# Relative attention on one Trainium2 core: turn and value order, and one maximum instruction for two tiles

## The chip, the cores and the metric

The kernel runs on 1 core of one Trainium2 chip. The metric is device time in microseconds (us). The engines of a core named here are PE (TensorE: matmuls and transposes, with the weight loads as PEld), DVE (VectorE), ACT (ScalarE), POOL (GpSimd) and SP (which only issues DMAs here). Each has its own queue and takes its instructions in order; they meet only at semaphores.

## The reference

Input `x` is (4, 1024, 256). Six layers follow one another, each on a layer norm of its input:

```python
x = x + 0.5 * L0_ffn(layernorm(x))      # binarised FFN
x = x + L0_attn(layernorm(x))           # local window + latent attention
x = x + 0.5 * L0_ffn(layernorm(x))
x = x + 0.5 * L1_ffn(layernorm(x))      # ternary weight, quantised input
x = x + L1_attn(layernorm(x))           # attention with relative positions
x = x + 0.5 * L1_ffn(layernorm(x))
```

The change is in `L1_attn` alone, with 16 heads of 16 features and 1024 tokens:

```python
rp = clip(key - query, -31, 31) + 31                      # 63 buckets
attn = q @ k.T + take(q @ rpe_k_table, rp) + take(k @ rpe_q_table, rp).T
attn = softmax(attn)
out = attn @ v + segment_sum(attn, rp, 63) @ rpe_v_table
return out @ w_proj.T + b_proj
```

## The kernel before, in words

The phase is `rel_attend` (from line 1632), written as one loop of steps on each engine, `for d in range(LAST)` with 291 steps. The order of all work is the order in which these five loops are written; nothing plans it at run time. 256 steps (`ND`) carry two **query tiles** each: tile t = 2d and 2d+1 is 128 queries of one head against all 1024 keys, with the relative bias in a band around the diagonal. Eight steps make a **round**: one half of the queries (512) of four heads; there are 32 rounds. In the text, r is d modulo 8.

What each tile is for:

- *Query side.* PE writes the scores of tile t into `SP[:, t % 2, :]`, two PSUM banks for each tile (`by_query`, 2060). DVE takes the negated maximum over the 1024 keys into one column of `nm` (`top`, 1915). ACT computes exp of the band alone, 160 or 192 columns, with that maximum as bias, into `Pb` (`band`, 1858). `by_query(t)` may overwrite its half of `SP` only when `band(t - 2)` has read it (line 2070).
- *The maxima as rows.* After eight steps the 16 columns of `nm` are transposed by PE (`turn`, kind "shift", 2158), split by DVE into two f16 rows (`turn_out`, 1935 and 1937), and ACT issues four DMAs that put them as two extra rows into `Q` (`shift_rows`, 1873 to 1882). From then on the key side of that round gets scores with the maximum subtracted already.
- *Key side.* Ten steps later (`JLAG`) PE computes the same scores with keys as rows, unit q = 2(d-10) and 2(d-10)+1, into `ST`, of which there is one buffer of two banks (`by_key`, 2031). ACT takes exp of all 128x1024 into `PT` (`probabilities`, 1849). `by_key(q)` waits until `probabilities(q - 1)` has emptied `ST` (line 2038). The first unit of a round also waits for the four DMAs of `shift_rows` (line 2040).
- *Values.* Twelve steps later (`VLAG`) PE multiplies `PT`, the transposed bands `PbT` and the summed diagonals `DT` with the values, into `PV` (`values`, 2101).
- *Turns.* One PSUM bank, `T`, serves transposes. Each step `turn_band` (2017) turns the bands of step d-2 and DVE copies them out (`band_out`, 1906). Some steps have one more use of `T` (`turn_of`, 1603): "shift" at r=0, "diag" at r=4 and r=6 (POOL's diagonal sums are transposed; ACT copies them to `DT`, line 1900), "back" at r=5 (the output `XOT`, which ACT copies from `PV` at r=4, line 1893), and 36 "tail" steps for the final projection.
- *POOL* stores bands to DRAM, reads back diagonals, and sums the low part (`lower`). *SP* loads queries, keys, bias and values ahead.

Order inside a step before the change. PE (2191 to 2198): `turn_band`, `by_key` A, both `by_query`, `by_key` B, `turn`, `values`. ACT (1884 to 1902): `probabilities` A, (r=1: `shift_rows` of the round before), `band(2d)`, (r=4: `XOT`), `probabilities` B, (`DT`), `band(2d+1)`. DVE (1984 to 1990): `band_out`, `moments`, `residual`, `top(2d)`, `top(2d+1)`, `turn_out`. A and B are the first and the second key unit of the step.

Of the kernel before, what the change touches and what calls it, by code (L numbers as in the profile page):

```python
# [7 lines left out]
ALU = mybir.AluOpType  # L8
ACT = mybir.ActivationFunctionType
AX = mybir.AxisListType  # L10
P = 128
B, S, D = 4, 1024, 256
# [10 lines left out]
ONE = 16  # L23
# [25 lines left out]
def sems(nc, ctx, prefix, names):  # L49

    s = {n: nc.alloc_semaphore(f"{prefix}_{n}") for n in names.split()}

    def clear():
        with nc.Block() as block:
            @block.sync
            def _(sp):
                for x in s.values():
                    sp.sem_clear(x)
        for x in s.values():
            nc.release_semaphore(x)  # L60
    ctx.callback(clear)
    return s
# [1519 lines left out]
NSLOT = 512  # L1582
ND = NSLOT // 2
NGRP = 16
NHALF = 32
JLAG, VLAG = 10, 12
# [5 lines left out]
def tile_of(t):  # L1592

    H, i = divmod(t, 16)
    return H // 2, 4 * (H % 2) + i // 4, i % 4


def band_slot(I, c):

    return c + (0 if I == 0 else 4 if I == TPB - 1 else 8 + 4 * (I % 2))  # L1600
# [31 lines left out]
def rel_attend(nc, G, A, wpT, BDv, rvd, QKD, END, GD, PW, VD, CST):  # L1632

    with ExitStack() as ctx:
# [6 lines left out]
        nm = sb("nm", [P, 2, 16])  # L1641
# [18 lines left out]
        SP = ps("S", [P, 2, S])  # L1660
# [3 lines left out]
        s = sems(nc, ctx, "a1c", "bp_in cst_in qk_in0 qk_in1 g_in0 g_in1 v_in0 v_in1 w_in0 w_in1 zero const S max band ST exp shift_tr shift_ev "  # L1664
                 "shift_in0 shift_in1 low lowt pw0 pw1 d_in vl Tb Tb_ev PV PVb diag_tr diag_ev diag O_ev back rs norm turn turn_ev "
                 "row proj res sums stat")
# [180 lines left out]
        @block.scalar  # L1847
        def _(act):
            def probabilities(q):
                if not 0 <= q < NSLOT:  # L1850
                    return
                act.wait_ge(s["ST"], ONE + q + 1)
                if q >= 8:
                    H, j = divmod(q - 8, 16)
                    act.wait_ge(s["PV"], ONE + 8 * H + 2 * (j // 4) + 2)
                nc.scalar.activation(PT[:, q % 8, :, :], ST[:, :, :], ACT.Exp).then_inc(s["exp"], 1)  # L1856

            def band(t):
                if t >= NSLOT:
                    return  # L1860
                n, I, c = tile_of(t)
                g = t // 4
                if c == 0 and g >= 2:
                    act.wait_ge(s[f"pw{g % 2}"], 16 * (g // 2))
                    act.wait_ge(s["Tb"], ONE + 2 * (g - 1))
                    act.wait_ge(s["low"], ONE + g - 1)
                w0, w1 = (32 if I == 0 else 0), (160 if I == TPB - 1 else GW)
                col = 4 * c + I % 4
                act.wait_ge(s["max"], ONE + t + 1)
                nc.scalar.activation(Pb[:, band_slot(I, c), w0:w1], SP[:, t % 2, I * P - 32 + w0:I * P - 32 + w1], ACT.Exp,  # L1870
                                     bias=nm[:, t // 16 % 2, col:col + 1]).then_inc(s["band"], 1)

            def shift_rows(H):
                n, qh = divmod(H, 2)
                act.wait_ge(s["shift_ev"], ONE + 2 * H + 2)
                if n >= 2:
                    act.wait_ge(s["ST"], ONE + 16 * (H - 3))
                for g in range(2):
                    for e in range(2):
                        r = 64 * g + 54 + e  # L1880
                        act.dma_start(Q[r:r + 1, n % 2, qh, :, :].rearrange("r c t -> r (c t)"), mhl[:, H % 2, e, :]
                                      ).then_inc(s[f"shift_in{H % 2}"], 16)

            for d in range(LAST):
                probabilities(2 * (d - JLAG))
                if d % 8 == 1 and 9 <= d <= 8 * NHALF + 1:
                    shift_rows(d // 8 - 1)
                band(2 * d)
                if d % 8 == 4 and 20 <= d < 20 + 8 * NHALF:
                    H = (d - 20) // 8  # L1890
                    act.wait_ge(s["PVb"], ONE + 4 * H + 4)
                    act.wait_ge(s["back"], ONE + H)
                    nc.scalar.activation(XOT[:, :], PV[:, :], ACT.Copy).then_inc(s["O_ev"], 1)
                probabilities(2 * (d - JLAG) + 1)
                turn = turn_of(d)
                if turn and turn[0] == "diag":
                    k = turn[1]
                    act.wait_ge(s["diag_tr"], ONE + k + 1)
                    act.wait_ge(s["diag"], ONE + k)
                    nc.scalar.activation(DT[:, :, :].rearrange("p k q -> p (k q)"), T[:, :], ACT.Copy  # L1900
                                         ).then_inc(s["diag_ev"], 1)
                band(2 * d + 1)

        @block.vector
        def _(dve):
# [6 lines left out]
                    dve.wait_ge(s["PVb"], ONE + (e - RING) // 2 + 1)  # L1912
                nc.vector.tensor_copy(PbT[:, e % RING, :], T[0:BW, :]).then_inc(s["Tb_ev"], 1)  # L1913

            def top(t):
                if t >= NSLOT:
                    return
                n, I, c = tile_of(t)
                dve.wait_ge(s["S"], ONE + t + 1)
                if t >= 32 and t % 16 == 0:  # L1920
                    dve.wait_ge(s["shift_tr"], ONE + t // 16 - 1)
                col = 4 * c + I % 4
                nc.vector.tensor_reduce(nm[:, t // 16 % 2, col:col + 1], SP[:, t % 2, :], AX.X, ALU.max,  # L1923
                                        negate=True).then_inc(s["max"], 1)

            def turn_out(d):
# [57 lines left out]
            for d in range(LAST):  # L1984
                band_out(d)
                moments(d)
                residual(d)
                top(2 * d)
                top(2 * d + 1)
                turn_out(d)  # L1990
            dve.wait_ge(s["stat"], ONE + NT)

# [1 line left out]
        def _(pe):  # L1994
# [17 lines left out]
            def last_turn_out(d):  # L2012
                for e in range(d - 1, max(d - 9, -1), -1):
                    if turn_of(e):
                        return turned_out(e)
# [133 lines left out]
            def turn(d):  # L2149
                use = turn_of(d)  # L2150
                if not use:
                    return
                kind, k = use
                pe.wait_ge(s["Tb_ev"], ONE + min(max(d - 1, 0), ND))
                last_turn_out(d)
                if kind == "shift":
                    pe.wait_ge(s["max"], ONE + 16 * (k + 1))
                    nc.tensor.transpose(T[0:16, 0:P], nm[:, k % 2, :], G.ident[:, :]).then_inc(s["shift_tr"], 1)
                if kind == "diag":
                    H = k // 2  # L2160
                    pe.wait_ge(s["d_in"], 64 * (H + 1))
                    pe.wait_ge(s["low"], ONE + 4 * (H + 1))
                    for i in range(2):
                        for pair in range(2):
                            at = 256 * i + P * pair
                            ins = nc.tensor.transpose(T[:, at:at + P],
                                                      Dt[:, H % 2, 2 * (k % 2) + i, 2 * pair:2 * pair + 2, :]
                                                      .rearrange("p h m -> p (h m)"), G.ident[:, :])
                    ins.then_inc(s["diag_tr"], 1)
                if kind == "back":  # L2170
                    pe.wait_ge(s["O_ev"], ONE + k + 1)
                    for i in range(4):
                        ins = nc.tensor.transpose(T[:, P * i:P * i + P], XOT[:, P * i:P * i + P], G.ident[:, :])
                    ins.then_inc(s["back"], 1)
                if kind == "tail":
                    b, j = divmod(k, len(TURNS))
                    if j < TPB:
                        pe.wait_ge(s["norm"], ONE + 8 * b + 7 + j // 4)
                        for q in range(KD):
                            ins = nc.tensor.transpose(T[:, q * P:q * P + P], xo[:, j, q * P:q * P + P], G.ident[:, :])  # L2180
                    if j >= 1:
                        pe.wait_ge(s["turn_ev"], ONE + k)
                        for q in range(KD):
                            ins = mm(T[:, D:2 * D], xoT[:, (j - 1) % 2, q * P:q * P + P], wpT[:, q, :], q == 0, q == KD - 1)
                    ins.then_inc(s["turn"], 1)
# [5 lines left out]
            for d in range(LAST):  # L2191
                turn_band(d)
                by_key(2 * (d - JLAG))
                by_query(2 * d)
                by_query(2 * d + 1)
                by_key(2 * (d - JLAG) + 1)
                turn(d)
                values(d)


# [58 lines left out]
```

## Time and profile before

| | |
|---|---|
| median of 3 runs | 2990.21 us (2980.34 to 2998.96) |
| profiled execution | 2981.21 us, its span 2979.5 us |
| mean granted TensorE clock | 0.895 |
| PE busy | 2259.6 us (76%) |
| DVE busy | 1689.0 us (57%) |
| ACT busy | 1230.9 us (41%) |
| POOL busy | 802.1 us (27%) |
| `L1923` maxima, DVE, x512 | 602.5 us busy, mean 1218 ns |
| `L1856` exp of the key side, ACT, x512 | 522.8 us busy, mean 1021 ns |

How to read it: the span is the time from the first to the last instruction of that execution. Busy is the time in which an engine ran at least one instruction; PE overlaps its matmuls, so that their durations add up to more than their stretch. A releaser in square brackets ("idle before <- who") is the instruction whose semaphore came last before the engine went on. "L1923" is line 1923 of the kernel; most matmuls of this phase go through one helper and have line 1996.

### The profile page before, as it was taken

How to read it: one execution, taken by the hardware profiler on the slowest of the kernel's cores; microseconds unless marked ns; L12 is line 12 of the kernel's file. 1: busy time of each engine (PE TensorE's matmuls, PEld its weight loads, DVE VectorE, ACT ScalarE, POOL GpSimd, SP SyncE). 2: the span in 40 equal slices, each digit the busy share in tenths (PEclk: the TensorE clock that was granted, in tenths of full speed). 3: DMA queues.
4: the chain of work that ended last, by engine and by line, in shares of the span. 5: the costliest groups of instructions: out<-in, count | busy, mean ns of one | idle time of the engine just before them, and what ended most of it. 6: DMA issues, size and time to landing. Idle time of an engine off the chain costs nothing. (4 is left out here: it accounts for less than half of the span.)

```text
span 2979.5 us, 78928 instructions
## 1 busy us (share of the span) xinstructions
PE 2259.6 (76%) x33368; PEld 1428.1 (48%) x33368; DVE 1689.0 (57%) x2810; ACT 1230.9 (41%) x1845; POOL 802.1 (27%) x1486
## 2 busy tenths in 40 slices
PE   0595888888869527859967787887878788888874
PEld 0363556555546413439964444444444444444433
DVE  5675453535357754423326666676667666766637
ACT  0472222121247501113213555555555555556544
POOL 0002000000000030000005555655665555546620
PEclk7798999999989768879985999999999999999986
DMA  2000000000000010133345344333343443333201
GB/s 86 1 1 22 17 8 10 15 3 16 2 1 1 4 26 21 35 131 118 111 132 129 109 108 108 102 82 104 107 112 105 107 112 102 99 100 107 79 27 61
DMA packets 231855, 195.25 MB, mean 66 GB/s; under 512 B 139920, under 2 KB 217438, under 8 KB 230238
## 3 DMA queue, kind: packets, MB, share of 16 engines
q1 hardware_dynamic: 211038, 122.95, 15.6%
q0 software_dynamic: 16384, 66.86, 6.8%
q8 instruction: 262, 4.29, 0.6%
q10 hardware_dynamic: 4096, 0.53, 0.1%
q14 instruction: 75, 0.61, 0.1%
HBM read 91.69 MB, written 93.88 MB: 62 GB/s over the span
## 5 line engine op out<-in xcount | busy, mean ns | idle before, releaser
L1923 DVE TENSOR_REDUCE a1c_nm<-a1c_S 128x1 f32<-128x1024 f32 x512 | 602.5, 1218 | 156.5 <-PE a1c_S L1996 155.6
L1856 ACT ACTIVATE a1c_PT<-a1c_ST 128x1024 f32<-128x1024 f32 x512 | 522.8, 1021 | 300.0 <-PE a1c_ST L1996 298.4
L1806 POOL TENSOR_TENSOR a1c_lt<-a1c_lt 128x128 f32<-128x128 f32 (+5 forms) x896 | 338.5, 378 | 70.2
L1913 DVE COPY a1c_PbT<-a1c_T 96x512 f32<-96x512 f32 x256 | 175.7, 686 | 300.4 <-PE a1c_T L2028 300.2
L1870 ACT ACTIVATE a1c_Pb<-a1c_S,a1c_nm 128x192 f32<-128x192 f32 (+1 forms) x512 | 213.7, 417 | 311.5 <-DVE a1c_nm L1923 289.7
L2028 PE MATMUL a1c_T<-ident,a1c_Pb 128*96 128x128 f32 x1024 | 175.4, 298 | 87.9 <-ACT a1c_DT L1900 53.3
L1996 PE MATMUL a1c_ST<-a1c_Q,a1c_KR 57*128 57x256 f16 (+5 forms) x1088 | 189.0, 297 | 69.0 <-DMA a1c_Q<-a1c_mhl 41.6
L1081 POOL PARTITION_ALL_REDUCE b_wall<-b_wsum x2 | 0.8, 406 | 808.3 <-DVE b_wsum L1126 808.3
L1996 PE MATMUL a1c_S<-a1c_KR,a1c_Q 54*32 54x512 f16 (+13 forms) x2816 | 190.2, 326 | 30.7 <-DMA a1c_KR<-a_consts 29.2
L2028 PEld LDWEIGHTS a1c_T<-ident,a1c_Pb 128*96 128x96 f32 x1024 | 108.0, 134 | 220.1 <-issue 161.9
L1996 PE MATMUL a1c_ST<-a1c_Q,a1c_KL 57*128 57x128 f16 (+3 forms) x960 | 163.5, 281 | 61.8 <-ACT a1c_PT L1856 38.9
L1996 PE MATMUL a1c_S<-a1c_KL,a1c_Q 54*32 54x512 f16 (+11 forms) x3136 | 204.6, 345 | 0.6 <-ACT a1c_Pb L1870 0.4
L1807 POOL TENSOR_TENSOR a1c_lt<-a1c_Pb,a1c_low 128x640 f32<-128x640 f32 x128 | 198.7, 1553 | 2.6
L1996 PE MATMUL a1c_S<-a1c_Gx,ident 64*32 64x96 f32 (+2 forms) x4352 | 193.9, 250 | 0.0
L1543 DVE TENSOR_TENSOR a1b_G<-a1b_k,a1b_G 128x256 f32<-128x256 f32 x192 | 72.6, 420 | 167.5 <-PE a1b_k L1575 167.5
L1996 PE MATMUL a1c_PV<-a1c_PT,a1c_VL 128*17 128x512 f32 (+3 forms) x1280 | 142.8, 520 | 29.1 <-issue 29.1
L1575 PE MATMUL a1b_k<-a_TKH,a_KL 128*128 128x64 f16 x768 | 144.4, 228 | 0.0
L1575 PE MATMUL a1b_k<-a_TKL,a_KH 128*128 128x64 f16 x768 | 144.3, 227 | 0.0
L1575 PE MATMUL a1b_k<-a_TKH,a_KH 128*128 128x64 f16 x768 | 144.1, 227 | 0.0
L1795 POOL DMA_DIRECT2D a_band<-a1c_Pb x128 | 74.5, 582 | 257.3 <-ACT a1c_Pb L1870 248.8
L1996 PEld LDWEIGHTS a1c_S<-a1c_Gx,ident 64*32 64x32 f32 x4352 | 133.0, 114 | 16.5 <-issue 1.6
L1996 PE MATMUL a1c_PV<-a1c_PT,a1c_VU 128*17 128x512 f32 (+3 forms) x1280 | 137.3, 503 | 0.0
(329 smaller groups left out, 5018.7 us busy)
## 6 DMA issues: line engine op xcount, KB each, us to landing
a_band<-a1c_Pb POOLq DMA_DIRECT2D x128, 384.0 KB, 3.4
a_bias<-a1b_G SPq DMA_DIRECT2D x8, 3072.0 KB, 11.5
a1c_Gx<-a_bias SPq DMA_DIRECT2D x128, 192.0 KB, 3.8
a1c_Dt<-a_band POOLq DMA_DIRECT2D x128, 126.0 KB, 3.2
a1c_Q<-a_qk SPq DMA_DIRECT2D x192, 64.0 KB
a1c_Vw<-a_values SPq DMA_DIRECT2D x64, 102.0 KB, 2.3
a1c_KL<-a_qk SPq DMA_DIRECT2D x96, 64.0 KB
a1c_KR<-a_qk SPq DMA_DIRECT2D x96, 64.0 KB
```

Of the source, the lines that this page charges most:

```text
L1081: nc.gpsimd.partition_all_reduce(wall[:, :], wsum[:, :], P, bass.bass_isa.ReduceOp.add).then_inc(s["wall"], 1)
L1543: ins = nc.vector.tensor_tensor(g, pk[:, x % 4, :].rearrange("p (x h r) -> p h r x", x=8, h=2)[:, h, :, :], g, ALU.add)
L1575: ins = mm(pk[:, x % 4, 64 * e:64 * e + 64], a[:, bass.ds(m, 1), key:key + 32 * (P - 1) + 1:32].rearrange("p k t -> p (k t)"), w[:, bass.d ...
L1795: pool.dma_start(PW[b * S + I * P:b * S + I * P + P, 4 * hq:4 * hq + 4, :], Pb[:, at:at + 4, :]).then_inc(s[f"pw{g % 2}"], 16)
L1806: add = lambda o, x, y: nc.gpsimd.tensor_tensor(o, x, y, ALU.add)
L1807: step(pool, nc.gpsimd.tensor_tensor(lt[:, :, :], Pb[:, at:at + 4, 0:160], low[:, :].unsqueeze(1).to_broadcast([P, 4, 160]), ALU.mult), c)
L1856: nc.scalar.activation(PT[:, q % 8, :, :], ST[:, :, :], ACT.Exp).then_inc(s["exp"], 1)
L1870: nc.scalar.activation(Pb[:, band_slot(I, c), w0:w1], SP[:, t % 2, I * P - 32 + w0:I * P - 32 + w1], ACT.Exp, bias=nm[:, t // 16 % 2, col: ...
L1913: nc.vector.tensor_copy(PbT[:, e % RING, :], T[0:BW, :]).then_inc(s["Tb_ev"], 1)
L1923: nc.vector.tensor_reduce(nm[:, t // 16 % 2, col:col + 1], SP[:, t % 2, :], AX.X, ALU.max, negate=True).then_inc(s["max"], 1)
L1996: return nc.tensor.matmul(out, w, x, start=start, stop=stop, skip_group_check=True)
L2028: ins = nc.tensor.transpose(T[0:BW, at:at + P], Pb[:, band_slot(I, c), BW * ch:BW * ch + BW], G.ident[:, :])
```

## The change

Five things differ, all in `rel_attend`.

- PE: `turn(d)` goes ahead of `by_key` B instead of after it.
- ACT: the copy to `XOT` goes from after `band(2d)` to the head of the step. The copy to `DT` goes ahead of `band(2d)`. So the order is: `XOT`, `probabilities` A, `DT`, `band(2d)`, `probabilities` B, `shift_rows`, `band(2d+1)`.
- ACT: `shift_rows` of a round is issued in the step of its transpose (r=0) instead of one step later (r=1), behind `probabilities` B instead of behind `probabilities` A.
- DVE: `top` is one instruction for both tiles of a step. It reads 128 x 2 x 1024, writes two columns of `nm` that are four apart, and waits for both query tiles.
- The semaphore `max` counts steps instead of tiles. So `band(2d)` waits for the maxima of both tiles.

```diff
 (ACT)
-                act.wait_ge(s["max"], ONE + t + 1)
+                act.wait_ge(s["max"], ONE + t // 2 + 1)
...
             for d in range(LAST):
-                probabilities(2 * (d - JLAG))
-                if d % 8 == 1 and 9 <= d <= 8 * NHALF + 1:
-                    shift_rows(d // 8 - 1)
-                band(2 * d)
                 if d % 8 == 4 and 20 <= d < 20 + 8 * NHALF:
...
                     nc.scalar.activation(XOT[:, :], PV[:, :], ACT.Copy).then_inc(s["O_ev"], 1)
-                probabilities(2 * (d - JLAG) + 1)
+                probabilities(2 * (d - JLAG))
                 turn = turn_of(d)
                 if turn and turn[0] == "diag":
...
                     nc.scalar.activation(DT[:, :, :].rearrange("p k q -> p (k q)"), T[:, :], ACT.Copy
                                          ).then_inc(s["diag_ev"], 1)
+                band(2 * d)
+                probabilities(2 * (d - JLAG) + 1)
+                if turn and turn[0] == "shift":
+                    shift_rows(turn[1])
                 band(2 * d + 1)
 (DVE)
-            def top(t):
-                if t >= NSLOT:
+            def top(d):
+                if d >= ND:
                     return
-                n, I, c = tile_of(t)
-                dve.wait_ge(s["S"], ONE + t + 1)
-                if t >= 32 and t % 16 == 0:
-                    dve.wait_ge(s["shift_tr"], ONE + t // 16 - 1)
+                n, I, c = tile_of(2 * d)
+                dve.wait_ge(s["S"], ONE + 2 * d + 2)
+                if d >= 16 and d % 8 == 0:
+                    dve.wait_ge(s["shift_tr"], ONE + d // 8 - 1)
                 col = 4 * c + I % 4
-                nc.vector.tensor_reduce(nm[:, t // 16 % 2, col:col + 1], SP[:, t % 2, :], AX.X, ALU.max,
+                nc.vector.tensor_reduce(nm[:, d // 8 % 2, col:col + 5:4], SP[:, :, :], AX.X, ALU.max,
                                         negate=True).then_inc(s["max"], 1)
...
-                top(2 * d)
-                top(2 * d + 1)
+                top(d)
                 turn_out(d)
 (PE)
-                    pe.wait_ge(s["max"], ONE + 16 * (k + 1))
+                    pe.wait_ge(s["max"], ONE + 8 * (k + 1))
...
                 by_query(2 * d)
                 by_query(2 * d + 1)
+                turn(d)
                 by_key(2 * (d - JLAG) + 1)
-                turn(d)
                 values(d)
```

## Rows read from the trace of the kernel before

**Rows 1.** Busy time of every engine from 1603.29 to 2849.71 us.

```profile
core 0: us, PE busy (x) PEld busy (x) DVE busy (x) ACT busy (x) POOL busy (x), PEclk, DMA share, GB/s
1603.29:2849.71 1246.42, 1011.85 (x18873) 564.31 (x18861) 826.96 (x988) 700.97 (x1081) 730.39 (x1385) 0.93 0.38 102
```

**Rows 2.** Waits, 1600 to 2840 us: engine line waited for: total us, times, longest us.

```profile
PE a1c_ST L1996 <- DMA a1c_Q<-a1c_mhl: 62.6, 30, 4.1
...
PE a1c_T L2028 <- ACT a1c_DT L1900: 52.3, 56, 5.1
...
ACT a1c_Pb L1870 <- POOL a1c_Dt L1806: 18.2, 8, 5.0
```

**Rows 3.** DVE, order of time, an ordinary step: start us, us, engine line op.

```profile
2100.34 0.69 DVE L1913 COPY a1c_PbT<-a1c_T 96x512 f32<-96x512 f32 x1 [1.04 <-PE a1c_T L2028]
2101.22 2.36 DVE L1923 TENSOR_REDUCE a1c_nm<-a1c_S 128x1 f32<-128x1024 f32 x2 [0.19 <-PE a1c_S L1996]
```

**Rows 4.** ACT, order of time, the same stretch and the step after it.

```profile
2102.48 0.42 ACT L1870 ACTIVATE a1c_Pb<-a1c_S,a1c_nm 128x192 f32<-128x192 f32 x1 [0.78 <-DVE a1c_nm L1923]
2102.80 1.01 ACT L1856 ACTIVATE a1c_PT<-a1c_ST 128x1024 f32<-128x1024 f32 x1
2103.70 0.42 ACT L1870 ACTIVATE a1c_Pb<-a1c_S,a1c_nm 128x192 f32<-128x192 f32 x1
...
2106.51 0.59 ACT L1893 ACTIVATE a1c_XOT<-a1c_PV 128x512 f32<-128x512 f32 x1
...
2107.89 0.61 ACT L1900 ACTIVATE a1c_DT<-a1c_T 128x512 f32<-128x512 f32 x1
```

**Rows 5.** PE (matmuls), order of time, the same step.

```profile
2100.24 0.34 PE L1996 MATMUL a1c_ST<-a1c_Q,a1c_KR 57*128 57x128 f16 x2
...
2101.76 0.34 PE L1996 MATMUL a1c_ST<-a1c_Q,a1c_KR 57*128 57x128 f16 x2 [0.23 <-ACT a1c_PT L1856]
...
2103.87 0.39 PE L1996 MATMUL a1c_ST<-a1c_Q,a1c_KR 57*128 57x256 f16 x2
```

**Rows 6.** DVE instructions by shape: count, busy us, mean ns, idle before.

```profile
L1923 DVE TENSOR_REDUCE a1c_nm<-a1c_S 128x1 f32<-128x1024 f32 x512 | 602.5, 1218 | 156.5 <-PE a1c_S L1996 155.6
...
L677 DVE TENSOR_REDUCE a_mt<-a_R 128x16 f32<-128x2048 f32 x32 | 73.4, 2293 | 72.0 <-PE a_R L855 72.0
...
L1969 DVE TENSOR_TENSOR x<-a1c_row,x 128x256 f32<-128x256 f32 x32 | 21.6, 675 | 0.1
```

**Rows 7.** DVE, order of time, a step with the turn of the maxima.

```profile
2085.56 2.36 DVE L1923 TENSOR_REDUCE a1c_nm<-a1c_S 128x1 f32<-128x1024 f32 x2 [0.18 <-PE a1c_S L1996]
...
2088.13 0.28 DVE L1937 TENSOR_TENSOR a1c_mhl<-a1c_T,a1c_mhl 16x128 f16<-16x128 f32 x1
```

**Rows 8.** ACT, order of time, its DMA issue in the step after.

```profile
2089.60 2.62 ACTq L1881 DMA_DIRECT2D a1c_Q<-a1c_mhl  x4
2092.27 0.42 ACT L1870 ACTIVATE a1c_Pb<-a1c_S,a1c_nm 128x192 f32<-128x192 f32 x1 [1.70 <-DVE a1c_nm L1923]
```

**Rows 9.** PE, order of time, the second query tile, and the wait for the maxima.

```profile
2085.27 0.39 PE L1996 MATMUL a1c_S<-a1c_KR,a1c_Q 54*32 54x448 f16 x4
...
2086.11 0.23 PE L1996 MATMUL a1c_ST<-a1c_Q,a1c_KL 57*128 57x128 f16 x1 [0.23 <-ACT a1c_PT L1856]
...
2095.60 0.34 PE L1996 MATMUL a1c_ST<-a1c_Q,a1c_KR 57*128 57x128 f16 x2 [2.80 <-DMA a1c_Q<-a1c_mhl]
```

**Rows 10.** The DMA of line 1881, from issue to landing.

```profile
DMA to landing us min/median/max: 1.6/2.7/5.4
```

**Rows 11.** DVE, order of time, steps 2 and 8, before ACT has key-side work.

```profile
1586.28 2.36 DVE L1923 TENSOR_REDUCE a1c_nm<-a1c_S 128x1 f32<-128x1024 f32 x2
...
1603.89 2.34 DVE L1923 TENSOR_REDUCE a1c_nm<-a1c_S 128x1 f32<-128x1024 f32 x2
```

**Rows 12.** Other stretches: PE busy share against the granted clock.

```profile
0.00:200.00 200.00, 97.46 (x637) 67.26 (x638) 125.13 (x327) 73.50 (x110) 0.82 (x7) 0.83 0.10 33
200.00:400.00 200.00, 151.16 (x2244) 96.36 (x2242) 100.00 (x180) 64.46 (x82) 19.17 (x29) 0.92 0.06 15
```

## The prediction

> **What bounds the kernel now.** I read the page first: nothing outside the relative attention is touched, so only that stretch matters. The windows view then takes it from the band copy of step 8 to that of step 256, which is 248 steps in 1246.42 us, 5.03 us a step; PE is busy 81% of it, DVE 66%, ACT 56% at a clock of 0.93 [rows 1]. PE is nearest to the bound, so the next view is what PE waits for. In 30 rounds it waits 62.6 us for the DMAs that bring the maxima into `Q`, and 52.3 us for the copy to `DT`; ACT waits 18.2 us for POOL's diagonal sums [rows 2]. The new order touches the first two. So the question is what the new order makes late instead, and for that the timelines of one step are laid side by side.
>
> The step to look at is an ordinary one. Its first key unit starts on PE at 2100.24, the next step's at 2103.87: 3.63 us [rows 5]. DVE runs the two maxima from 2101.22, 2.36 us for both [rows 3]. ACT starts `band(2d)` 1.26 us after that, which is the first maximum alone (mean 1.22 us [rows 6]) and 0.04 us; in other steps this link is 0.12, I take 0.08. `probabilities` B starts 0.32 us later, lasts 1.01 and ends at 2103.81; the next key unit starts 0.06 us after it [rows 4, 5]. It must: `ST` has one buffer. So a chain already closes over each step: maximum, `band(2d)`, `probabilities` B, next key unit, first query tile, next maximum. Today it is 3.6 us, because it holds only the first of two maxima and the first of two query tiles, and the mean step of 5.03 us hides it.
>
> **The merged maximum.** The one row of this shape of work is a reduction of 2048 PSUM columns, 2293 ns, against 2.36 us for the pair: 0.07 us less on DVE [rows 3, 6]. It writes 16 values where this one writes 2; I take 2.29 and 2.36 as ends, and 2.29. DVE is not the bound, so the 0.07 us x 256 = 18 us are worth nothing as busy time. What costs is the semaphore: `band(2d)` now waits for all of it, and it can only start when both query tiles are in PSUM. From the start of the key unit to the end of the second tile PE needs 1.29 us (2101.76 less its idle 0.23, less 2100.24 [rows 5]).
>
> The new chain, link by link: merged maximum 2.29; link 0.08; `band(2d)` to `probabilities` B 0.32; `probabilities` B 1.01; link 0.06; key unit and both query tiles 1.29; link to DVE 0.06 (taken equal to the other). Sum **5.11 us**. Nothing in the new order breaks it: `band(2d)` stays ahead of `probabilities` B, B ahead of the next key unit, and that ahead of the next query tiles. It holds in every step from 10 to 255 (246 steps); 5.11 is above today's mean, so every step that took 3.6 to 5.0 us is stretched to it. With the links at their smallest it is 5.07, at their largest with 0.1 more on PE 5.25.
>
> Here a page has another figure for the merging: Perfetto Trace Analysis of the Trainium skill, section Optimizing Scalar/DVE Operations, gives an overhead of about 125 ns for each DVE instruction on PSUM. By it the merged one would save 0.125 us, not 0.07, and the sum below would be an estimated 14 us smaller; the 2293 ns row decides for 0.07.
>
> **`shift_rows` one step earlier.** Gain: the DMAs are issued in step r=0 and needed in r=2. Issue takes 2.62 us on ACT's queue and landing 1.6 to 5.4 us [rows 8, 10]; they start 2.84 us after the maximum's start in r=0 and are needed 6.66 + 3.76 = 10.42 us after it (both worked out here and above), so with 2.62 and the median landing of 2.7 they are in at 8.2 and only the slowest landings are late: the 62.6 us wait goes. Cost: DVE has the two rows ready 0.49 us after the pair of maxima (2088.41 against 2087.92 [rows 7]). `probabilities` B runs by then, and the four issues overlap with it, as today's do with A; but `band(2d+1)` stands behind them on ACT. From the maximum's start: 2.29 + 0.49 + 0.06 + issue 2.62 + 0.05 + band 0.42 (start at 2092.27, end of issue 2092.22 [rows 8]) + 0.06 = 5.99 us, when the next second query tile may start. That tile takes 0.61 us (2085.27 to 2086.11 less 0.23 [rows 9]), then 0.06: the next maximum starts after 6.66 us instead of 5.11. **1.55 us x 31 rounds = 48 us.** Bounds: 0, if the issue stays in cover, and 48.
>
> **`XOT`, `DT`, `turn`.** The two copies of 0.6 us [rows 4] and PE's turn now fall where ACT and PE wait 2.3 us for DVE; the copies leave the place between the maxima and `band(2d+1)`. Cost nothing. `XOT` at the head waits for the values of the step before, which PE ends well within the chain, since PE needs 3.63 us for a step with the 0.23 us wait in it. If the chain were shorter, `turn` ahead of key unit B would delay B and the values. The 52.3 us wait goes too: `turn_band` waits for a `DT` that is done 1 us earlier. But neither gain can be cashed, because the chain of 5.11 us already contains no wait of these kinds. On SP and POOL nothing is moved.
>
> **Small terms.** The first ten steps have no key side. Steps 2 to 8 take 2.94 us each now [rows 11]; there the chain is 2.29 + 0.08 + 0.32 + 0.42 + 0.06 + 0.61 + 0.06 = 3.84, so eight of them cost 7 us. In 32 steps the residual (0.68 us [rows 6]) and statistics stand on DVE between the band copy and the maximum, with 0.19 us of slack now [rows 3] and 0.39 more when the maximum waits for the second tile: 0.3 us each, 10 us (0 to 20). Of the 18.2 us behind POOL I keep 9 (0 to 18), since slower steps give POOL time.
>
> **Sum.** 246 x 5.11 = 1257; steps 8 and 9, 8; shift 48; DVE 10; POOL 9: 1332 us against 1246, so +86, and 7 at the start: +93 us. The profiled execution took 2981.2 us (span 2979.5): 3074. The median of the three runs is 2990.2, 9 above it; I go half of that up: **3078 us**.
>
> **Rivals.**
>
> *The waits go and the chain stays in cover (faster).* PE is the busiest engine; if its order still set the pace, 62.6 + 52.3 us would come off: 2866 us. It decides from the point where the chain is under about 4.9 us a step, that is if the next key unit did not have to wait for `probabilities` B. For it: PE's 81%, and that these are PE's largest waits on other engines. Against: the chain, five durations that all stand in rows. The same page, section Optimization Strategy, says to take the engine with the highest occupancy and to make what ends its gaps start sooner; here that advice points to this rival. Chance 0.07.
>
> *Only the merging counts (no change).* The moved waits turn into others of the same size and DVE's 18 us come off or not: 2963 to 2985. Against it the same chain. Chance 0.06.
>
> *The chain binds, the four issues stay in cover.* 48 us less: 3030. For it, ACT runs B during 1 us of the issue; against, today's `band(2d)` starts only after the issue, 1.70 us idle [rows 8]. Chance 0.10.
>
> *The chain binds and the clock falls.* PE would be busy about 76% of a step. If it were granted 0.83 as at the start of the kernel (busy 49%) and not 0.92 as in the next stretch (busy 76%) [rows 12], 1.29 us would become 1.45: 246 x 0.16 = 39 us more, 3117. Chance 0.05; the second of these rows is the nearer.
>
> *Forecast:* 0.72.
>
> **The numbers.** The range must reach the two cases beside the forecast, and the bounds of the links (5.07 to 5.25: -10 to +34 us): 3012 to 3130. That leaves the faster and the unchanged case out, 0.13, and some of the tails. No change means within 1%, 30 us, which is about what a measurement can tell. Faster by over 1%: 0.07; within: 0.06; slower: 0.87.
>
> **What would show it.** Right: the starts of the merged maximum 5.1 us apart in nearly all steps, whatever r, and about 6.6 apart from r=0 to r=1; no wait of PE for the DMA of the maxima (today 2.80 us in the example [rows 9]); the first key unit of every step starting 0.06 us after `probabilities` B; PE busy 77% or less there. Wrong: merged maxima of over 2.4 us, starts 4.9 us or less apart, or a key unit that waits for something else.

## The result and the profile after

The changed kernel takes 3134.3 us (median of 4 runs) against 2989.1 us before: ratio 1.049, 95% interval 1.046 to 1.051. It is slower, as forecast, by 145 us where 88 were forecast, and it lies 4 us above the range.

The page of the kernel after: busy time by engine, the merged maximum, and the granted clock in 40 slices.

```profile
span 3133.4 us, 78596 instructions
...
PE 2336.7 (75%) x33292; PEld 1457.8 (47%) x33368; DVE 1673.2 (53%) x2554; ACT 1235.4 (39%) x1845; POOL 803.3 (26%) x1486
...
PEclk7797999999999668799858888898888888988886
...
L1923 DVE TENSOR_REDUCE a1c_nm<-a1c_S 128x2 f32<-128x2048 f32 x256 | 586.9, 2293 | 417.1 <-PE a1c_S L1995 416.6
```

DVE is busy 16 us less (1689.0 before), as the merging should give: 256 maxima at 2293 ns. The clock row has nines in the stretch of the relative attention before (0.90 to 0.97 in stretches of 100 us from 1700 to 2800 us), and now mostly eights (0.84 to 0.91).

The waits of the stretch, kernel after (engine line waited for: us, times, longest us):

```profile
ACT a1c_Pb L1870 <- DVE a1c_nm L1923: 504.2, 223, 4.0
...
PE a1c_ST L1995 <- ACT a1c_PT L1856: 182.2, 211, 3.0
...
ACT a1c_Pb L1870 <- POOL a1c_Dt L1806: 2.2, 1, 2.2
```

The wait of 62.6 us for the DMAs of the maxima and that of 52.3 us for `DT` [rows 2] are gone. In their place ACT waits 504 us for the maxima, 246 before, and PE waits 182 us for ACT's exp, 54 before.

One plain step, r=4 to r=5 of round 13, counted from 0 (the rows of before are [rows 3 to 5]). DVE, ACT and PE of the kernel after, each in order of time:

```profile
2186.43 2.29 DVE L1923 TENSOR_REDUCE a1c_nm<-a1c_S 128x2 f32<-128x2048 f32 x1 [0.95 <-PE a1c_S L1995]
...
2191.59 2.29 DVE L1923 TENSOR_REDUCE a1c_nm<-a1c_S 128x2 f32<-128x2048 f32 x1 [2.27 <-PE a1c_S L1995]
```

```profile
2188.84 0.42 ACT L1870 ACTIVATE a1c_Pb<-a1c_S,a1c_nm 128x192 f32<-128x192 f32 x1 [1.27 <-DVE a1c_nm L1923]
2189.16 1.02 ACT L1856 ACTIVATE a1c_PT<-a1c_ST 128x1024 f32<-128x1024 f32 x1
2190.06 0.42 ACT L1870 ACTIVATE a1c_Pb<-a1c_S,a1c_nm 128x192 f32<-128x192 f32 x1
```

```profile
2187.97 0.64 PE L2027 MATMUL a1c_T<-ident,a1c_Pb 128*96 128x128 f32 x4
2190.23 0.39 PE L1995 MATMUL a1c_ST<-a1c_Q,a1c_KR 57*128 57x256 f16 x2 [1.62 <-ACT a1c_PT L1856]
```

The chain of the prediction, link by link: maximum 2186.43; `band(2d)` 2.41 us later; `probabilities` B 0.32 later, for 1.02; next key unit 0.05 after its end, at 2190.23, PE idle 1.62 us before it; next maximum 1.36 later. Sum 5.16 us, forecast 5.11. The intervals between the starts of the maxima from step 8 on have a median of 5.17 us from r=2, 5.16 from r=4 and 5.19 from r=6. ("From r=2" means from the maximum of a step with r=2 to the next one.)

### The profile page after: what moved, and what is told of

Read it like the earlier page. It is cut to its first block and busy times, and to the rows that moved or that the text cites. A ratio compares the mean times of both kernels' runs of the same rounds, so it can differ in the third digit from the quotient of the medians.

```text
span 3133.4 us, 78596 instructions
## 1 busy us (share of the span) xinstructions
PE 2336.7 (75%) x33292; PEld 1457.8 (47%) x33368; DVE 1673.2 (53%) x2554; ACT 1235.4 (39%) x1845; POOL 803.3 (26%) x1486
## 5 line engine op out<-in xcount | busy, mean ns | idle before, releaser
L1923 DVE TENSOR_REDUCE a1c_nm<-a1c_S 128x2 f32<-128x2048 f32 x256 | 586.9, 2293 | 417.1 <-PE a1c_S L1995 416.6
L1995 PE MATMUL a1c_ST<-a1c_Q,a1c_KR 57*128 57x256 f16 (+5 forms) x1088 | 196.4, 309 | 99.2 <-ACT a1c_PT L1856 97.4
L2027 PE MATMUL a1c_T<-ident,a1c_Pb 128*96 128x128 f32 x1024 | 186.3, 311 | 64.8 <-ACT a1c_Pb L1870 49.7
L1995 PE MATMUL a1c_PV<-a1c_PT,a1c_VU 128*17 128x512 f32 (+3 forms) x1280 | 167.6, 602 | 0.0
L1995 PEld LDWEIGHTS a1c_ST<-a1c_Q,a1c_KL 57*128 57x128 f16 (+1 forms) x960 | 74.6, 99 | 165.1 <-ACT a1c_PT L1856 140.4
```

What stands on the lines that cost most here:

```text
L1923: nc.vector.tensor_reduce(nm[:, d // 8 % 2, col:col + 5:4], SP[:, :, :], AX.X, ALU.max, negate=True).then_inc(s["max"], 1)
L1995: return nc.tensor.matmul(out, w, x, start=start, stop=stop, skip_group_check=True)
L2027: ins = nc.tensor.transpose(T[0:BW, at:at + P], Pb[:, band_slot(I, c), BW * ch:BW * ch + BW], G.ident[:, :])
```

## The experiments

Each kernel is compared with the kernel before on the same chip. Mean intervals are taken from step 8 to step 255. Code cuts leave lines out at "...". Line numbers in their profiles are shifted where lines were added.

**The merging alone.** The kernel before, with `top(d)` and the semaphore by steps, and the old orders:

```diff
-                top(2 * d)
-                top(2 * d + 1)
+                top(d)
...
-                act.wait_ge(s["max"], ONE + t + 1)
+                act.wait_ge(s["max"], ONE + t // 2 + 1)
```

> The kernel before with one thing of the change: a single maximum for both tiles, and the semaphore by steps; every order as before. Theory (chain: both maxima, band(2d), probabilities B, key unit, both query tiles): the chain of 5.16 us a step is closed by the merging alone, so this is slow too, and slower than the changed kernel, because XOT lies inside the chain at r=4 (+0.5 us a round), the copy to DT holds turn_band until 4.9 us after the maximum's start instead of 3.8 at r=4 and r=6 (+2.2), and the shift DMAs land late (+0.5), against 1.7 us for their place in the changed kernel: about +1.5 us x 31, 3180 us. Rival (the new order costs, not the merging): 2990 us, as before.

Measured: 3277.3 us, ratio 1.099 (1.094 to 1.105). The merging alone costs 291 us, twice what the whole change does. The interval from r=4 to r=5, ACT of this kernel (2176.66 to 2184.51 between maxima):

```profile
2179.07 0.42 ACT L1870 ACTIVATE a1c_Pb<-a1c_S,a1c_nm 128x192 f32<-128x192 f32 x1 [2.29 <-DVE a1c_nm L1923]
2179.39 0.59 ACT L1893 ACTIVATE a1c_XOT<-a1c_PV 128x512 f32<-128x512 f32 x1
2179.87 1.02 ACT L1856 ACTIVATE a1c_PT<-a1c_ST 128x1024 f32<-128x1024 f32 x1
2180.77 0.61 ACT L1900 ACTIVATE a1c_DT<-a1c_T 128x512 f32<-128x512 f32 x1
2181.25 0.44 ACT L1870 ACTIVATE a1c_Pb<-a1c_S,a1c_nm 128x192 f32<-128x192 f32 x1
```

`XOT` stands inside the chain and `DT` behind it; the band transposes wait for `DT`. The mean interval is 7.86 us from r=4 and 7.42 from r=6; the expected costs put on the chain of 5.16 give 6.8 and 6.3. So the direction is right, and the price of the copies was too low by about 1.1 us each time, some 70 of the 97 us that the expected 3180 us is short. In this step the transposes behind them ran at half clock (0.50 granted from 2181.5 to 2182.7 us; at full clock they take 0.64 us):

```profile
2181.54 1.09 PE L2027 MATMUL a1c_T<-ident,a1c_Pb 128*96 128x128 f32 x4
```

**The order alone.** The changed kernel with the two maxima:

```diff
-                top(d)
+                top(2 * d)
+                top(2 * d + 1)
...
-                act.wait_ge(s["max"], ONE + t // 2 + 1)
+                act.wait_ge(s["max"], ONE + t + 1)
```

> The changed kernel with the two separate maxima of before, so only the new orders of PE and ACT and the earlier shift_rows. Theory (chain): 3.6 us a step as before, under PE's own time; the waits for the shift DMAs (62.6 us) and for DT (52.3 us) go, the place of the issue in r=0 costs some 1.2 us a round (37 us): 2912 us. Rival (the order costs): over 3050 us.

Measured: 2994.4 us, ratio 1.003 (1.001 to 1.005). The rival (the order costs) falls, but 82 us of the expected gain are missing. Waits of this kernel, 1620 to 2860 us:

```profile
POOL a1c_VL L1833 <- DMA a1c_VU<-a_values: 193.3, 14, 14.9
...
ACT a1c_Pb L1870 <- POOL a1c_Dt L1806: 76.1, 14, 6.8
ACT a1c_Pb L1870 <- issue: 69.0, 25, 3.7
```

ACT waits 76.1 us for POOL's diagonal sums, 18.2 before [rows 2]. POOL itself waits 193 us for the value DMA of the next group (line 1833), and the bands queue behind that. The same kernel with this POOL work later (below) is 102 us faster, so POOL accounts for all that is missing. The issue on ACT, which holds `band(2d+1)`, costs what was expected: the interval from r=1 is 7.52 us instead of 6.32, 1.2 us a round.

**`probabilities` B ahead of `band(2d)`**, with the merged maximum:

```diff
-                band(2 * d)
                 probabilities(2 * (d - JLAG) + 1)
+                band(2 * d)
```

> The changed kernel with probabilities B ahead of band(2d) on ACT, nothing else. Theory (chain): the key unit of the next step no longer hangs behind the merged maximum; what is left of the chain is maximum 2.29, link 0.08, band 0.32, band(2d+1) 0.42, link 0.06, second query tile 0.61, link 0.06 = 3.84 us, under PE's own 4.1 to 4.3 us; the shift issue in r=0 costs 2.5 us a round: 2990 - 31 x 4.1 = 2868 us, faster than both kernels. Rival (the wait for both query tiles ahead of the maximum, or the PE work, sets the step, not probabilities B): 3050 to 3134 us.

Measured: 3006.5 us, ratio 1.008 (1.005 to 1.011): 128 us less than the changed kernel, from one line. DVE of this kernel, steps r=3 to r=5:

```profile
2077.04 2.29 DVE L1923 TENSOR_REDUCE a1c_nm<-a1c_S 128x2 f32<-128x2048 f32 x1 [1.03 <-PE a1c_S L1995]
...
2080.91 2.29 DVE L1923 TENSOR_REDUCE a1c_nm<-a1c_S 128x2 f32<-128x2048 f32 x1 [0.56 <-PE a1c_S L1995]
...
2084.82 2.29 DVE L1923 TENSOR_REDUCE a1c_nm<-a1c_S 128x2 f32<-128x2048 f32 x1 [0.59 <-PE a1c_S L1995]
```

The intervals are 3.87 and 3.91 us; the chain without `probabilities` B was worked out at 3.84. So B behind the merged maximum is what sets 5.16. The expected time of 2868 us was missed by 138 us. Single steps from r=6 take over 9 us behind POOL, and the kernels further down put POOL's share at 85 us (2945.5 to 2861.0). Much of the rest is in steps that never reached the short chain: the interval from r=0 is 6.79 us, from r=1 5.53 and from r=5 4.97; what holds those from r=5 was not tried.

**`shift_rows` at its old place**, step r=1 behind `probabilities` A:

```diff
                 probabilities(2 * (d - JLAG))
+                if d % 8 == 1 and 9 <= d <= 8 * NHALF + 1:
+                    shift_rows(d // 8 - 1)
...
-                if turn and turn[0] == "shift":
-                    shift_rows(turn[1])
```

> The changed kernel with shift_rows at its old place: step r=1, behind probabilities A. Theory (the issue on ACT holds band(2d+1) in r=0 by 1.5 us a round): the interval from r=0 to r=1 falls from 6.85 to 5.2 us; the DMAs, in cover of the merged maximum in r=1, land about 0.7 us late for the key unit of r=2: 31 x 1.0 = 30 us less than the changed kernel, 3104 us. Rival (the earlier issue is free and only removed a wait): the wait of 62.6 us comes back, 3190 us.

Measured: 3109.2 us, ratio 1.043 (1.038 to 1.047), 25 us less than the changed kernel, with intervals of the two ratios that barely overlap (up to 1.0472, and from 1.0461). The traces show the trade: the interval from r=0 is 5.49 us instead of 6.83, that from r=1 6.26 instead of 5.67, and PE waits for the DMAs again, in 23 rounds:

```profile
PE a1c_ST L1995 <- DMA a1c_Q<-a1c_mhl: 39.6, 23, 4.3
```

**More work on PE.** In the wait before the first key unit, matmuls with zero weights (`zf`, a new tile that POOL sets to zero) add zeros to `PV`:

```diff
+            def filler(d):
+                if not 13 <= d < ND or d % 8 == 4:
+                    return
+                w = 256 if d % 2 == 0 else 512
+                for c in range(4):
+                    mm(PV[32 * c:32 * c + VW, 0:w], zf[:, :], wpT[:, :, :].rearrange("p k q -> p (k q)")[:, 0:w], False, False)
...
             for d in range(LAST):
                 turn_band(d)
+                filler(d)
```

> The changed kernel with more work on PE: between turn_band and the first key unit, where PE waits for probabilities B, four matmuls with zero weights add zeros to PV (512 columns ahead of odd steps, 256 ahead of even ones, none ahead of r=4). Theory (what the steps have beyond the chain of 5.16 us comes from PE at half clock after its wait, which makes values and turn_band late): the granted clock of the stretch rises from 0.87 to 0.92 or more, the interval from r=5 to r=6 falls from 5.66 towards 5.2, and the time falls by 10 to 35 us although PE does more: about 3110 us. Rival (the extra is PE's own work or its order): the filler only adds, 3134 us or more.

Measured: 3109.9 us, ratio 1.041 (1.038 to 1.045); the intervals of the two ratios do not meet, so more PE work made the kernel faster, by 24 us. The kernel after, and then the one with the filler, 1700 to 2900 us:

```profile
core 0: us, PE busy (x) PEld busy (x) DVE busy (x) ACT busy (x) POOL busy (x), PEclk, DMA share, GB/s
1700.00:2900.00 1200.00, 953.67 (x16525) 513.58 (x16523) 709.99 (x658) 615.68 (x941) 631.12 (x1193) 0.87 0.35 95
```

```profile
1700.00:2900.00 1200.00, 1006.03 (x18314) 503.81 (x18316) 726.44 (x669) 625.63 (x958) 648.16 (x1225) 0.99 0.36 97
```

The granted clock goes from 0.87 to 0.99. The mean interval from r=1 falls from 5.67 to 5.24 us, from r=3 from 5.50 to 5.28, from r=0 from 6.83 to 6.63; from step 8 to step 255 the maxima are 1351 us apart instead of 1376. One part of the expectation was missed: from r=5 it falls from 5.65 to 5.53 only, not towards 5.2. There nearly every step now takes 5.54 to 5.55 us; the 1.05 us of added matmuls are the likely reason, not a tested one.

**The issue on SP's queue**, on top of B ahead: the four DMAs of `shift_rows` go behind `load_bias` in SP's loop.

```diff
                     load_bias(n, 1)
+                    shift_rows(2 * n - 1)
...
                     load_bias(n + 1, 0)
+                shift_rows(2 * n)
...
+            shift_rows(31)
```

> The kernel with probabilities B ahead of band(2d), and the four DMAs of shift_rows issued by SP's queue instead of ACT's. Theory (the issue on ACT holds band(2d+1)): the interval from r=0 to r=1 falls from 6.83 to about 4.2 us, 31 x 2.6 = 80 us less; part comes back as waits for POOL, which is late once in every second round: 2940 us. Rival (the hold is from the DVE rows or PE, not the issue): 3000 us.

Measured: 2945.5 us, ratio 0.986 (0.982 to 0.989). The interval from r=0 falls from 6.79 to 4.93 us, where 4.2 were expected. ACT's wait for POOL's sums is 70.0 us there.

**`left_values` later**, on top of the last, and on top of the order alone:

```diff
-                if g % TPB == 4 and g // TPB + 1 < NGRP:
+                if g % TPB == 7 and g // TPB + 1 < NGRP:
```

> As the one with SP's issue, and POOL's left_values for the next group three query blocks later (block 7 instead of 4), so that POOL does not stand waiting for that group's value DMA while bands pile up. Theory (the faster step now runs into POOL): ACT's waits for POOL's sums go, no interval from r=6 or r=7 over 6 us; 8 steps take some 34.5 us against 40.2 before: 2990 - 31 x 5.7 = 2813 us. Rival (POOL's own work is the bound, not its place in the order): no gain over the last, 2940 us.

Measured: 2861.0 us, ratio 0.957 (0.954 to 0.960). No row of ACT waiting for POOL's sums is left; the interval from r=6 is 3.93 us, 6.29 in the kernel before this edit. 48 us of the expected gain are missing: the mean intervals of eight steps add up to 36.0 us instead of 34.5, with 5.06 from r=0, 4.89 from r=1, 5.01 from r=5 and 4.62 from r=7.

> The order-only kernel (two separate maxima) with left_values three blocks later. Theory (its missing gain went into 76 us of ACT's waits for POOL's sums): 60 to 76 us less, about 2925 us. Rival (the gain went into the issue in r=0 alone, and POOL's wait is hidden): 2994 us.

Measured: 2892.1 us, ratio 0.967 (0.963 to 0.971), 102 us less than the order alone, where 60 to 76 were expected. POOL's place had taken all of the 82 us missing there and more.

> The kernel before with left_values three blocks later and nothing else. Theory (that place cost 18.2 us of ACT's waits in the slow order, and 76 us in the faster one): 18 us less than before, 2970 us. Rival (worth the same in any order): 2910 us.

Measured: 2959.6 us, ratio 0.988 (0.984 to 0.993), 32 us less: more than the 18 us of the wait row, but a third of what the same line is worth in the new order (102 us). In the order with the faster steps more of POOL's waiting for the value DMA shows.

**Both repairs with two maxima.** The order alone with SP's issue and late `left_values`; then the same with B ahead of `band(2d)`:

> The order-only kernel (two separate maxima) with left_values later and the four shift DMAs on SP's queue. Theory (issue on ACT is what is left of the loss at r=0 and r=1, 7.2 us where a step of the chain is 3.6 to 4): about 2 to 2.5 us a round less than the same kernel with the issue on ACT: 2892 - 31 x 2.3 = 2820 us. Rival (PE's own time is the bound already): 2880 us.

> The kernel with probabilities B ahead of band(2d), issue on SP and late left_values, but with the two separate maxima of before. Theory (the chain with the merged maximum is 3.84 us a step, with two it is 3.6 or less, and PE's own 3.5 to 5.0 us now set most steps): the steps r=2, 3, 4 and 6 fall from 3.92 to 3.6 us, so 4 x 0.3 x 31 = 37 us less than with the merged one: 2824 us. Rival (the instruction saved on DVE counts once the chain is short): 2861 us or more.

Measured: 2806.3 us, ratio 0.938 (0.934 to 0.942), and 2791.3 us, ratio 0.932 (0.926 to 0.938). Expected were 2820 and 2824. The last has the lowest median, 6.8% under the kernel before, but the intervals of the two overlap, so that B ahead of `band(2d)` gives nothing clear here. Against its twin with the merged maximum (0.957) the two maxima give 70 us, where 37 were expected: even with the chain at its shortest, the instruction saved is worth less than an early start. PE of the fastest kernel is the first engine of this row:

```profile
1650.00:2700.00 1050.00, 943.28 (x18554) 536.31 (x18548) 813.45 (x967) 709.60 (x1068) 714.46 (x1348) 0.98 0.43 118
```

PE is busy 90% of the stretch at 0.98, against 81% before [rows 1]; it is now close to setting the pace.

## Why the prediction was right and where it was wrong

**The mechanism was right.** The semaphore that waits for both maxima closes a chain of 5.16 us (5.11 forecast), no step from 10 on is shorter than 5.03, and both waits of [rows 2] went without being cashed. The experiments take it apart: the merging alone 1.099, the order alone 1.003, both 1.049. The new order is not a cost; it halves what the merging costs, since it takes `XOT` and `DT` out of the chain (the intervals from r=4 and r=6 are 7.86 and 7.42 us in the old order, 5.24 and 5.21 in the new one). Taking B out of the chain gives 3.9 us in the steps that nothing else holds.

**`shift_rows`: right.** 1.55 us a round were forecast. The mean interval from r=0 is 6.83, less 5.16: 1.67 us. DVE and ACT in the step that opens round 12, kernel after:

```profile
2119.80 2.29 DVE L1923 TENSOR_REDUCE a1c_nm<-a1c_S 128x2 f32<-128x2048 f32 x1 [1.22 <-PE a1c_S L1995]
...
2122.31 0.28 DVE L1937 TENSOR_TENSOR a1c_mhl<-a1c_T,a1c_mhl 16x128 f16<-16x128 f32 x1
...
2126.55 2.29 DVE L1923 TENSOR_REDUCE a1c_nm<-a1c_S 128x2 f32<-128x2048 f32 x1 [2.48 <-PE a1c_S L1995]
```

```profile
2122.50 1.02 ACT L1856 ACTIVATE a1c_PT<-a1c_ST 128x1024 f32<-128x1024 f32 x1
2122.62 2.44 ACTq L1881 DMA_DIRECT2D a1c_Q<-a1c_mhl  x4
2125.11 0.40 ACT L1870 ACTIVATE a1c_Pb<-a1c_S,a1c_nm 128x160 f32<-128x160 f32 x1 [1.59 <-issue]
```

The rows are ready at 2122.59, the issue takes until 2125.06, `band(2d+1)` starts at 2125.11 where it would have been due at 2123.4, and the next maximum comes at 2126.55. Put back at its old place it takes a net 25 us off the changed kernel.

**The sum was short, and the step that failed is PE's clock, which the sum put at nothing.** The span grew by 153.9 us, 93 forecast. From the starts of the maxima (the forecast counts 248 steps between band copies, the measured column the 247 between maxima; that leaves 1 to 2 us over):

| term | forecast | measured |
|---|---|---|
| ahead of the first maximum (1580.6 to 1592.8) | 0 | +12 |
| steps 0 to 7 | +7 | +13 |
| chain, 246 steps | 5.11 us | 5.16 us: 12 more |
| r=0, 31 rounds | 48 | 52 |
| all else above the chain, steps 8 to 254 | 19 (residual 10, POOL 9) | 50: 27 tail steps 17; r=1, 3 and 5 outside them 28; the rest 5 |
| after the last maximum | 0 | -6 |

The first is no effect of the change: four of the experiments with the merged maximum have their first one at 1581 to 1585, two at 1592. I had put the median half of 9 us above the profiled execution for such differences. The chain's 0.05 us a step is mostly its first link, from the maximum to `band(2d)`: 0.12 us in this step, where I had taken 0.08.

"All else" holds the step that failed. The prediction had "the chain binds and the clock falls" as a rival, at 0.05, because the stretch with 76% busy had 0.92 [rows 12]; the mean share hid how the wait lies. PE now stands idle before the first key unit (1.62 us in the step above), and in some steps what follows is at half clock. Windows of the kernel after in a step from r=5 that took 6.07 us:

```profile
2149.00:2152.00 3.00, 3.00 (x45) 1.27 (x43) 1.70 (x3) 1.65 (x3) 0.00 (x0) 0.64 0.02 5
2152.00:2155.00 3.00, 3.00 (x62) 1.92 (x66) 1.80 (x2) 1.60 (x2) 2.82 (x3) 1.00 0.33 131
```

```profile
2149.21 1.48 PE L1995 MATMUL a1c_PV<-a1c_PT,a1c_VL 128*17 128x384 f32 x8
...
2151.92 0.64 PE L2027 MATMUL a1c_T<-ident,a1c_Pb 128*96 128x128 f32 x4
2152.49 0.39 PE L1995 MATMUL a1c_ST<-a1c_Q,a1c_KL 56*128 56x512 f16 x1
```

The same values in the same kernel at full clock, and ACT's `probabilities` B of the slow step:

```profile
2187.19 0.84 PE L1995 MATMUL a1c_PV<-a1c_PT,a1c_VL 128*17 128x384 f32 x8
```

```profile
2150.46 1.02 ACT L1856 ACTIVATE a1c_PT<-a1c_ST 128x1024 f32<-128x1024 f32 x1
```

In the first 3 us the granted clock is 0.64, a mixture of 0.5 (1.2 GHz) and 1; the values of 128x384 take 1.48 us, where they take 0.84 at full clock. `turn_band` comes at 2151.92 and the key unit at 2152.49, when `probabilities` B had ended at 2151.48: PE's own order is longer than the chain for this step. It is the same over the whole stretch: of the 31 steps from r=5, 14 were granted 1.00 and took 5.10 to 5.11 us, 17 were granted 0.72 to 0.81 and took 5.45 to 6.28. The filler shows that the clock is the cause, not only a companion: with it at 0.99 the time falls by 25 us although PE does more, 6 of them from r=0 and 19 of these 50, and from r=1 and r=3 outside the tail steps the mean is 5.05 and 5.12 us, so nothing above the chain is left. I had applied the lower clock to the 1.29 us of PE in the chain; its price lies in values and `turn_band`, which at half clock no longer fit beside the chain.

So of the 61 us by which the sum was short, the clock holds about half: some 28 here (of which the filler gives 19 back, net of its own work) and the 6 of steps 0 to 7 below. The rest is 12 in the chain, some 7 in the tail steps and the chance 12 ahead of the first maximum, and POOL gives some 7 back. The tail steps are not the clock's alone: nine of them take 6.6 to 6.8 us whether 0.77 or 1.00 was granted (6.56 to 6.68 with the filler), where I had 0.3 us over the chain each; which of their DVE and PE work holds them was not tried alone. The range ended at 3130 because it took the falling clock (3117) or the largest links (34 us), not both; measured, both came in part.

Of the signs named, the first key unit starts within 0.1 us after `probabilities` B in about three steps of four, not in every one, and PE is busy 79% of 1700 to 2900 us, not 77% or less: at half clock its work takes longer.

Steps 0 to 7 are the same error. I worked their chain out at 3.84 us with a second query tile of 0.61 us from a row at full clock; the clock there is 0.50 in both kernels, and the two query tiles take 1.7 us together (1604.63 to 1606.3) where they take 1.0 at full clock (2190.55 to 2191.5). The kernel after, then the one before:

```profile
1592.79:1629.57 36.78, 20.75 (x357) 13.92 (x357) 22.49 (x16) 5.76 (x16) 17.66 (x33) 0.50 0.58 135
```

```profile
1580.55:1603.89 23.34, 21.24 (x353) 11.99 (x345) 22.70 (x24) 6.63 (x16) 15.62 (x28) 0.50 0.80 186
```

**POOL: too high.** 9 us were kept of its 18.2 [rows 2]; 2.2 remain.

**The rival "the waits go and the chain stays in cover" (2866 us)** shows what was to be had: without the merging and with its two follow-up waits taken away, 2806. The advice to find an engine's gaps and to make what ends them start sooner (Trainium skill, Perfetto Trace Analysis, section Optimization Strategy) pointed to real gaps; alone it brought nothing (1.003), since POOL's place and the issue on ACT took the gain. The Trainium skill, Perfetto Trace Analysis, section Optimizing Scalar/DVE Operations, also says that where these engines are not saturated but cause bubbles elsewhere, breaking instructions up may let work finish sooner. DVE is busy 66% here [rows 1], and the runs agree: two maxima instead of one give 2.4 to 9% in three orders (2791 against 2861, 2994 against 3134, 2986 against 3277 us).

## What to carry to other kernels

Merging two instructions also merges their semaphores: before it is done, follow the first consumer of the first half to the end of its loop, and compare that chain with the mean step, not with the busy time saved. Work issued in order behind a late wait (here `probabilities` B, which needed nothing from the maximum) should go ahead of it: that gave 128 us with the merged maximum, and nothing clear with two. A wait that is removed is cashed only if the next engines in line, here POOL and the DMA issue on ACT, have room. And idle time placed ahead of PE's work can cost more than the idle time itself: look at the granted clock step by step, not at its mean.

## What the runs showed of the hardware

Work added to PE in its waits made a kernel faster: some 6 us of matmuls a round (1.05 us ahead of odd steps, 0.63 ahead of even ones in its trace), 24 us less in all, at a granted clock of 0.99 instead of 0.87. A reduction over 2048 PSUM columns takes 2293 ns with 2 outputs as with 16 [rows 6]. Four DMA issues on ACT's queue (2.44 us, 2122.62 to 2125.06) ran beside the ACTIVATE that was issued ahead of them (2122.50), but the next one started only at 2125.11.
